# Values of the first attention taken two key blocks at a time, in a mixed order of blocks; the first stage's sums split over two engines

## What is computed

```python
# layer 0: differential attention, 16 heads, 4 key heads, two maps each (m = 0, 1), 16 wide
q1, q2 = rope(q1), rope(q2);  k1, k2 = rope(k1), rope(k2)
a1 = softmax(q1 @ k1.T / 4 + causal);  a2 = softmax(q2 @ k2.T / 4 + causal)
out = groupnorm((a1 - lam * a2) @ v) @ Wo          # all heads
g = silu(mxfp4(xn) @ mxfp4(W).T + bias)
# layer 1: 16 heads of causal attention, 16 wide; 16 experts with 4 chosen, and shared ones
```

## Time and profile before

| | |
|---|---|
| three runs, us | 801.05, 803.25, 800.54; median 801.05 |
| the profiled execution, us | 801.43, of which 799.7 is the span of the core's instructions |
| busy in the span | PE 94%, DVE 70%, ACT 53%, POOL 46% |
| mean granted TensorE clock | 0.988 of full speed |

### The profile page before, as it was taken

How to read it: one execution, slowest core, us unless ns; L and a number is a source line. 1 busy time by engine, 2 the same in 40 slices (tenths; PEclk the granted TensorE clock), 3 DMA queues, 4 the chain that set the end, 5 groups by cost and what they waited for, 6 DMA issues and landing times. The chain is left out here.

```text
span 799.7 us, 12969 instructions
## 1 busy us (share of the span) xinstructions
PE 752.7 (94%) x3791; PEld 373.1 (47%) x3791; DVE 557.1 (70%) x1420; ACT 426.1 (53%) x915; POOL 368.3 (46%) x706
## 2 busy tenths in 40 slices
PE   4888999999999999999899899999899999999995
PEld 3342222222222223223655333333378888888883
DVE  3788877877777777723774888887287665666666
ACT  2432566666666666674233257777644553555552
POOL 1661666674334433431233123445366664566664
PEclk9999999999999999999999999999999999999997
DMA  6393740020011001102029146454542221222221
GB/s 201 118 293 119 182 108 16 19 65 15 15 43 48 16 16 45 40 21 61 0 85 235 65 122 165 153 171 151 152 115 67 66 64 51 53 66 60 64 67 56
DMA packets 56532, 69.41 MB, mean 87 GB/s; under 512 B 13089, under 2 KB 35010, under 8 KB 56467
## 3 DMA queue, kind: packets, MB, share of 16 engines
q1 hardware_dynamic: 56392, 68.65, 30.3%
q10 hardware_dynamic: 80, 0.07, 0.0%
HBM read 46.37 MB, written 15.44 MB: 77 GB/s over the span
## 5 line engine op out<-in xcount | busy, mean ns | idle before, releaser
L852 ACT ACTIVATE top<-ps 128x512 f32<-128x512 f32 (+3 forms) x384 | 170.6, 491 | 124.1 <-PE ps L770 124.1
L770 PE MATMUL ps<-mid 99*128 99x512 bf16 (+3 forms) x576 | 181.0, 331 | 5.5 <-ACT mid L852 4.7
L886 DVE CUSTOM_DVE_ANT_0 ps<-ps,keep 128x512 f32<-128x512 f32 (+3 forms) x320 | 161.9, 530 | 26.0 <-PE ps L746 25.9
L746 PE MATMUL ps<-mid 96*128 96x512 bf16 (+3 forms) x512 | 166.0, 337 | 5.2 <-DVE top L886 1.0
L792 PE MATMUL ps<-top,mid 128*33 128x512 f32 (+3 forms) x768 | 160.9, 498 | 0.0
L1702 PE MATMUL ps<-xp,wp 128*128 128x512 f32 (+1 forms) x600 | 144.8, 390 | 1.0 <-DVE mid L1872 0.5
L770 PEld LDWEIGHTS ps<-mid 99*128 99x128 bf16 x576 | 53.8, 97 | 166.4 <-ACT top L852 103.2
L1702 PEld LDWEIGHTS ps<-xp,wp 128*128 128x128 f32 (+1 forms) x600 | 111.8, 187 | 25.7 <-POOL wp L1802 0.9
L986 POOL TENSOR_SCALAR_AFFINE_SELECT top<-top 128x128 f32<-128x128 f32 x256 | 71.7, 295 | 104.4 <-ACT top L852 102.4
L890 DVE TENSOR_REDUCE top<-ps 128x1 f32<-128x512 f32 x128 | 88.3, 690 | 32.8 <-PE ps L746 32.5
L852 ACT ACTIVATE mid<-ps 128x512 f32<-128x512 f32 (+1 forms) x192 | 81.3, 496 | 47.9 <-PE ps L770 46.7
(11 more groups left out here) (224 smaller groups left out, 862.3 us busy)
## 6 DMA issues: line engine op xcount, KB each, us to landing
mid<-part_scratch SPq DMA_DIRECT2D x9, 1152.0 KB, 8.7
part_scratch<-top SPq DMA_DIRECT2D x18, 384.0 KB, 3.0
mid<-combine_rows SPq DMA_DIRECT2D x48, 128.0 KB, 3.0
part_scratch<-top SPq DMA_DIRECT2D x18, 256.0 KB, 3.1
top<-in_w SPq DMA_DIRECT2D x6, 634.0 KB, 4.7
mid<-part_scratch SPq DMA_DIRECT2D x9, 384.0 KB, 4.1
top<-in_w SPq DMA_DIRECT2D x4, 640.0 KB, 7.3
top<-in_w SPq DMA_DIRECT2D x4, 633.0 KB, 5.1
```

What stands on the lines that cost most here:

```text
L746: nc.tensor.matmul(ps[:, s_bank(turn), 0:w], queries(pair, m)[0:PARTS, i * P:(i + 1) * P], keys(pair, m)[0:PARTS, c * 512:c * 512 + w], st ...
L770: nc.tensor.matmul(ps[:, ST_BANK + n % AHEAD, 0:w], keys(pair, m)[0:STACK, j * P:(j + 1) * P], queries(pair, m)[0:STACK, q0:q0 + w], start ...
L852: nc.scalar.activation(pr[:, n % RING, 0:w], ps[:, ST_BANK + n % AHEAD, 0:w], ACT.Exp, scale=0.25).then_inc(p_ready, 1)
L886: ins = nc.vector.tensor_tensor_reduce(bank, bank, msk[:, 512 - w:512], -1.0 if low else 1.0, 3e38 if low else -3e38, ALU.add, ALU.min if ...
```

## The change

It changes seven things, five of them in layer 0 alone. (1) Values are taken in groups of four blocks (two key blocks of both maps) in the first attention as in the second; the ring has nine places. (2) `SB` and `MB` of the first attention take their key blocks and query tiles from tables. (3) DVE makes the odd units' sums in the start, and its small work (mask tile, lambda, bias) stands ahead of the loop. (4) Eight filler matmuls instead of 18 end the start. (5) SP gathers the near maps before it waits for unit 4, and the far maps of the keys after the first pair's rows. (6) In both attentions, SP sends the next pair's rows before it reads the inverses of half 0. (7) POOL's `scale` moves from k = 8 to 10 (both layers), MXFP4's step 4 from 9 to 10, DVE's `combine` from 15 to 18.

```diff
-def score_blocks():
+def score_blocks(order):
...
-        for j in range(4 * c + 4):
+        for j in order[c]:
...
+KEYS0, QUERIES0 = ((0, 1, 3, 2), (1, 3, 6, 2, 7, 4, 5, 0)), (2, 3, 1, 0, 4, 7, 6, 5)
+KEYS1, QUERIES1 = (range(4), range(NT)), range(NT)
...
                     for u in range(SENT):
-                        sp.wait_ge(lo_ok, u + 1)
-                        written0(sp, u)
                         if u == 4:
                             near_maps0(sp, 4)
                             near_maps0(sp, 0)
+                        sp.wait_ge(lo_ok, u + 1)
+                        written0(sp, u)
                         if u == 5:
                             far_maps0(sp, 0)
-                        if u == 6:
-                            far_maps0(sp, 4)
...
-                        if u < len(UN):
+                        if u < len(UN) and u % 2 == 0:
                             pool.wait_ge(roped, u + 1)
...
+                            if u % 2 == 1:
+                                dve.wait_ge(roped, u + 1)
+                                if u >= 2:
+                                    dve.wait_ge(r1_ok, u - 1)
+                                nc.vector.tensor_tensor(qf[:, 1, :], tA[:, 1, :], tB[:, 1, :], ALU.add).then_inc(added[1], 1)
...
-                    for _ in range(18):
+                    for _ in range(8):
                         keep_busy(2)
...
-                RING, LAG = 8 if first else 9, 1
-
-                WIDE = 2 if first else 4
-                GROUPS = [(b, b + WIDE) for b in range(0, PAIR, WIDE)]
+                RING, LAG = 9, 1
+
+                GROUPS = [(b, b + 4) for b in range(0, PAIR, 4)]
...
-                QUANT_POOL = {9: 4, 12: 5, 17: 7, 19: 8, 21: 9, 23: 10}
+                QUANT_POOL = {10: 4, 12: 5, 17: 7, 19: 8, 21: 9, 23: 10}
...
-                                start, stop = j == 0, j == 4 * c + 3
+                                start, stop = j == order[c][0], j == order[c][-1]
...
-                            if first and h in (1, 2) and f > 0 and k == 15:
+                            if first and h in (1, 2) and f > 0 and k == 18:
                                 combine(dve, f - 1, h - 1)
...
-                            if h in (1, 2) and f > 0 and k == 8:
+                            if h in (1, 2) and f > 0 and k == 10:
                                 scale(pool, f - 1, h - 1)
...
                             if f > 0 and h == 0:
-                                inverses(sp, f - 1, 0)
+                                inverse_sent(sp, f - 1, 0)
                             if pair + 1 < N:
                                 rows(pair + 1)
+                            if f > 0 and h == 0:
+                                inverse_read(sp, f - 1, 0)
...
         def late0(sp, pair):
+            if pair == 0:
+                far_maps0(sp, 4)
```

More of the change, by code:

```diff
@@ L55, in score_blocks, with max_blocks @@
     return out
-def max_blocks():
+def max_blocks(order):
     out = []
-    for i in range(NT):
+    for i in order:
         for m in range(2):
@@ L241, in program @@
             stats, rstd, normed, ids = (sem(n, a) for n in ("stats", "rstd", "normed", "ids"))
-            x_tr, xT_ok, proj, roped, added = (sem(n, a) for n in ("x_tr", "xT_ok", "proj", "roped", "added"))
+            x_tr, xT_ok, proj, roped = (sem(n, a) for n in ("x_tr", "xT_ok", "proj", "roped"))
+            added = [sem(f"added{n}", a) for n in range(2)]
             q_mm, qs_ok = sem("q_mm", a), sem("qs_ok", a)
@@ L299, in _ @@
                             nc.gpsimd.tensor_tensor(qf[:, u % 2, :], tA[:, u % 2, :], tB[:, u % 2, :],
-                                                    ALU.add).then_inc(added, 1)
+                                                    ALU.add).then_inc(added[0], 1)
                         if u >= 2:
@@ L324, in _ @@
                         if u < len(UN):
-                            act.wait_ge(added, u + 1)
+                            act.wait_ge(added[u % 2], u // 2 + 1)
                             if u >= SLOTS:
@@ L376, in bias_part @@
                             link(nc.vector.tensor_tensor(bip[64:65, :], bir[64:65, :], bim[64:65, :], ALU.subtract))
+                    dve.wait_ge(ld_c, 112)
+                    nc.vector.tensor_copy(msk[:, 384:512], tri[:, :])
+                    for n in range(2):
+                        last = nc.vector.tensor_tensor(lp[:, n, :], lm[:, 2 * n, :], lm[:, 2 * n + 1, :], ALU.mult)
+                    link(last)
+                    nc.vector.tensor_reduce(ls[:, :], lp[:, :, :], AX.X, ALU.add).then_inc(lsum, 1)
+                    for n in range(7):
+                        bias_part(n)
                     for u in range(len(UN) + 1):
@@ L382, in _ @@
                             if u >= 2:
-                                dve.wait_ge(added, u - 1)
+                                dve.wait_ge(added[u % 2], u // 2)
                             b = 2 * (u % 3)
@@ L477, in attention @@
             READS = 32 if first else 16
+            order = KEYS0 if first else KEYS1
+            SB, MB = score_blocks(order), max_blocks(QUERIES0 if first else QUERIES1)
+            assert len(SB) == PAIR and len(MB) == PAIR
             LASTF = N // 4 - 1
@@ L1016, in _ @@
                                 mask(n)
-                            if not first and h == 0 and f > 0 and k in (8, 21):
-                                sum_halves(pool, f - 1, 0 if k == 8 else 1)
-                            if h in (1, 2) and f > 0 and k == 8:
+                            if not first and h == 0 and f > 0 and k in (10, 21):
+                                sum_halves(pool, f - 1, 0 if k == 10 else 1)
+                            if h in (1, 2) and f > 0 and k == 10:
                                 scale(pool, f - 1, h - 1)
```

5 lines of the change are left out of this document (removed).

## The result

The changed kernel takes **794.77 us** (median of 8 runs, 791.28 to 797.88); before, 8 runs of the same comparison gave 800.75. The ratio is 0.9919 (0.9901 to 0.9936): 6.0 us faster, where 19.9 were forecast, and outside the range of 775 to 793. One of e3's ten runs took 1,447 us and is left out of e3's ratio. The changed kernel's helpers lie four lines lower: plain scores L750, scores L774, values L796, transpose L764.

A forecast was written before the change was run, and what follows sets the result against it. PE was taken to bound the first attention's full pairs. Terms -19.1 - 1.0 + 5.6 - 3.2 - 2.2 = -19.9 us, from the profiled 801.43 us, gave 781.5 us; range 775 to 793.

The forecast's parts named there:

- 0.227 us for each change from bf16 to f32 and back: First attention, PE: cost per matmul type change; six fewer per pair over 14 pairs save 19.1 us.
- rival of a tax per matmul: Overhead belongs to each matmul, so grouping saves nothing and only the start gains: 796 us; chance 0.03.
- What the bursts cost: First attention's pairs: waits from values coming in groups of four, 0.4 us a pair, +5.6 us over 14 pairs.
- rival of costlier bursts: Bursts cost 0.8 to 1.3 us a pair, 11 to 18 us over 14 pairs: 787 to 794; chance 0.18.
- cost nothing: SP only issues, and what the gather could delay is the rows of pair 1, which have some 5 us: SP's moved rows and far-key gather: no cost, pair 1's rows having two groups of PE's work before use.
- those before 88.20 lie in a stretch where DVE ... sets the pace, so I count nothing: Changes saved before 88.20 us, where DVE is busy for 27.10 of 30.84 us: counted at 0.
- covered by a hair, in six pairs: POOL's scale behind the split: masks ready after 5.1 us, PE there after 5.3; a miss, 1.8 us, held by the 5.6.
- waits for nothing new: DVE's combine, three places later in the pair: no new wait, no cost counted.
- I count half, 1.0 us: First attention's end, no plain scores left: nine saved changes worth 2.0 us, half counted because PE waits for exponentials.
- The start: Start: shared sums bring units from 3.20 to 2.85 us apart, saving 3.2 us; ten fewer filler matmuls save 2.2 us.
- if that needs nothing that comes later: Start's end: condition on the fillers' 2.2 us, that the first attention's first matmul needs nothing arriving later; near maps expected earlier.

The follow-up runs named there:

- e3: Changed kernel without its attention part, so the kernel before with only the start's edits (groups of two, natural orders, old places); 799.68 us, ratio 0.9991.
- e2: Changed kernel with groups of two blocks again in the first attention, mixed order, start, gathers and places kept; 805.93 us, ratio 1.0072.
- e1: Kernel before with only groups of four blocks and nine ring places in the first attention, natural order of blocks; 806.81 us, ratio 1.0084.
- e4: Changed kernel with the gathers of the keys' far maps and the next heads' maps one pair later; 791.61 us, ratio 0.9889.
- e5: e4 plus keep-busy matmuls in pair 0, one behind each of 14 plain scores in five steps; 789.11 us, ratio 0.985.
- e6: e4 with POOL's scale put back from step 10 of the pair to step 8; 789.26 us, ratio 0.9845.
- e7: e4 with the last pairs' values, where no plain scores are left, done two at a time instead of four; 790.56 us, ratio 0.9859.
- e11: e6 with DVE's combine put back from step 18 to step 15 of the pair; 789.29 us, one run.
- e9: Changed kernel with the four edits of e4, e5, e6 and e7 together; 786.29 us, ratio 0.9819.
- e10: e9 with the transpose of the maxima put ahead of the values at step 13 instead of behind them; 790.7 us, ratio 0.9872.

## Why the prediction was wrong, point by point

- **"0.227 us for each change from bf16 to f32 and back"** held. e2 and the changed kernel differ by the groups alone: 18.46 against 17.58 in a plain pair, 0.88, which is 1.36 for six changes less the 0.48 of the next point. Two key blocks at 512 columns took 1.84, within the 0.99 + 0.86 that I named. (The rival of a tax per matmul should have stood at 801.6 and not at 796, since the bursts' 5.6 would have come on top; it failed either way.)
- **"What the bursts cost"**, 0.4 us a pair: 17.58 - 15.74 - 1.36 = 0.48 in plain pairs, right in size. By their starts, five matmuls of a plain pair come 0.06 to 0.13 us late, 0.45 in sum. What made it small, I had wrong: the comparison with the second attention in natural order said that order hardly mattered, and e1 shows 1.4 us of waits in natural order. The rival of costlier bursts (787 to 794) comes within 1 us of the measured time, but not by its mechanism; that would have been true without the mixed order.
- **"cost nothing: SP only issues, and what the gather could delay is the rows of pair 1, which have some 5 us"** failed. The use stood 5.48 us behind the transpose before and 3.68 after, because of the two groups that I counted between them only one stands there; the landing takes 3.3 in the best case, and 5.75 behind the far maps. Measured +2.8 instead of -0.96 at pair 1, of which e4 got all back. In e3 the same backlog gave back 2.4 us of the start.
- **"those before 88.20 lie in a stretch where DVE ... sets the pace, so I count nothing"** failed, by 3.1 us. No gain was right; but the stretch could lose. 0.3 us came ahead of the first transpose (17.15 against 16.81). In pair 0 DVE has 14.22 us to do between the transposes (e3, natural order: 13.42), and 0.8 stay with the clock at full level (14.84 against 14.03). The other 1.9 (16.76 against 14.84) went with the fall of the clock; e4 against e5 puts it at 1.2.
- **"covered by a hair, in six pairs"**: the scale itself missed by 0.08 us in the second pairs of a family (e6), and by far more behind the last transpose, which I had not counted: 0.38 us of wait with groups of four, 1.17 with groups of two (e7). The pairs with quotients lost 0.33 to 0.52 each, 2.1 us over five, mostly to the rows' slack and to `combine`, which "waits for nothing new": 0.24 (e11).
- **The last nine changes, "I count half, 1.0 us"** failed by 3.5 us. Two things cost there, and each hides behind the other. Without plain scores the bursts have no cover, and PE waits 1.8 us for exponentials (e4); and the `scale` ahead of the masks delays the values. Groups of two alone leave the end at 23.89 (e2) and 23.55 (e7), `scale` at k = 8 alone at 22.78 (e6). With both, e9 brings the end back to 21.63, against 21.26 before.
- **The start**, -3.2 - 2.2: the products' spacing is 2.89 us (9 of them in 26.0), as forecast (2.82 by the forecast's own three terms, 2.85 in its sum), and the fillers went; but "if that needs nothing that comes later" didn't hold, PE idles 2.23 us for POOL's last low parts. The term was 4.4, not 5.4. What the start gained, pair 1's rows took back until the maps were moved.

The sum of what was missed, 1.0 + 3.1 + 3.7 + 3.5 + 3.5 - 1.0 = 13.8, is the distance from 781.5 to the profiled 795.57, but for 0.3 (0.1 of it around the span). The mechanism was right and its size in the steady stretch too; the failed step is costing edits at nothing, or at a gain, in the passages where another engine or a transfer sets the pace.

What stays open is the fall of the clock in pair 0. It is there in all eight profiles with a mixed order and no fillers, in none of before, e1 and e3, and in none of the three with fillers. PE idles for DVE in both orders (before it is busy for 11.68 of 14.03 us at 1.00), so I can't say which of the gaps tips it. The Trainium skill, "TensorE: Matmul & The Clock Gate", section "A second HAM failure mode: psum-queue depth-cycling", says that short idles between groups of matmuls can make the clock fall. The waits of 0.24 and 0.27 us in pair 0 and e5's row at 1.00 agree with it; before's pair 0, with waits of up to 0.43 us for DVE and no fall, shows that such idles are not enough by themselves.

## What to carry to other kernels

When a stretch that one engine fills is shortened, compute for each transfer and each small helper in it the distance from its start to its use, before and after: here a slack of 2.2 us became 0.4, and every late transfer then showed. Bursts of work need cover from something else; where that runs out, at the first and last rounds of a pipeline, make the groups small again, and move helpers out of the way of what the last groups wait for. If an edit moves the mark by which a stretch is measured, compare places that are the same work in both kernels (e10). And a grouping and an order can each cost time apart (e1, the grouping, +6.3 us; e2, the order with the start, +5.4) and gain 6.0 together: try them as one.

## What the runs showed of the hardware

- A switch between bf16 and f32 matmuls (with the change of tile) costs 0.23 us there and back, once for a group of any length seen: a lone key block of 512 columns (0.85 us of stream) shows 1.05, four key blocks of 1,536 columns in sum (2.56 us) show 2.77. The change of type and that of tile were not tried apart.
- Fourteen short keep-busy matmuls in a stretch where PE waits for DVE made it 1.2 us shorter (16.05 to 14.84), with the granted clock at 1.00 where it was 0.79.
- Falls of the clock ahead of the last stage lasted from 3.4 to 10.2 us, and came not in each profile at the same places (the second attention: none, 3.4 or 6.8). That is some 1 us up or down from trace to trace, and the spread of the runs has room for it.
- Rows of 6 KB issued behind three gathers of some 2.7 MB in sum landed 5.75 us (after) and 7.78 us (e3) behind their transpose instead of 3.3, each within 0.5 us of the last gather's landing.
- In the changed kernel's start DVE's L408 takes 0.68 us, but 1.64 in the three units where POOL's L301 runs beside it (29.05, 35.21 and 41.36 us): sharing the sums did not end that.
